# Gated cross-attention with a mixture of experts on one core: five expert tiles multiplied at the end of the attention program

## The chip, the cores and the metric

The kernel runs on one core of a Trainium2 chip. The metric is the device time of one execution in microseconds (us). Engines are named as the profile names them: PE is TensorE (matmuls), PEld its weight loads, DVE is VectorE, ACT is ScalarE, POOL is GpSimd, SP is SyncE, which here issues most DMAs.

## The reference: what is computed

```python
x = x + tanh(g_xattn) * xattn(layernorm(x), ctx)        # x: 4 x 2048 x 512, ctx: 4 x 77 x 512, 16 heads
x = x + tanh(g_ffn)   * ffn(layernorm(x))

def ffn(x):                                             # 8192 tokens of 512
    probs = softmax(x @ gate_w.T + gate_b)              # 8 true experts and 2 null ones
    weights, selected = top_k(probs, 2)
    true = weights * (selected < 8)
    norm = true / (true.sum(-1) or 1)
    return sum_k norm[k] * (x @ expert_w[selected[k]] + expert_b[selected[k]])
```

## The kernel before

The program has three parts, each a block with one instruction stream per engine. An engine enters a block only when all five have left the one before (a barrier: POOL gathers the other four, then releases them; it has the line of the block's start, L598 at the end of attention).

`fold_context` multiplies the context with the projection weights once. `attend` then goes over 64 tiles of 128 tokens in 64 turns and four more (`tail`, i = 64 to 67). A turn i works on several tiles: PE makes the scores of tile i (L908), the weighted sum `mix` of tile i-2 (L923) and the gate logits of tile i-4 (L955); DVE makes the probabilities of i-1, adds the residual of i-3 (`x_out`, L1152) and normalizes it (`y`, L1169), for which POOL computes the reciprocal root (`y_rstd`, L1499, x_moments); ACT does the exponentials and the f16 halves; SP turns p and y by DMA transposes (L819, L824, L809). In each stretch every engine goes through its list strictly in order. Every four tiles (a group, 16 in all) DVE ranks the tokens by expert in spread-out steps (place_1 to place_8), and POOL scatters eight rows of 128 entries each into a table in HBM (L1597). `placed` holds the counts so far. At the very end PE sums the counts (`totals`, L1002), and DVE makes the list of expert tiles from them (`count_tiles`, `find_tiles`, from L1609).

`run_experts` works through that list, first for the tokens' smaller choice (0), then for the other (1), each in passes of five tiles (RING = 5): one pass always, up to a counted number inside, and a last one. Per tile SP fetches the 128 table entries (L1769), DVE writes the token numbers (L1940), POOL gathers the rows by an indirect DMA (L1799), ACT normalizes (L1908), PE turns the tile with four f32 transposes (L1862), ACT and DVE make two f16 halves, PE does twelve 128x512 matmuls (L1875), DVE adds the bias and scales (L1963, L1988), and POOL scatters the result (L1820). PE starts the block with 14 matmuls whose result is not used (`WARM`, L1854). Choice 0 gathers and scatters into the second half of each token's row of `comb`; tiles are 128 tokens of one expert, the last of each expert filled up.

What sets the order around the change are the written-out step functions: `step` and `tail` of each engine in `attend`, and the first lines of each engine in `run_experts`. Of POOL there:

```python
listing.scatter(pool, table, 1, 2, 1, 2)
pool.wait_ge(cleared, 1)
for j in range(LEAD):                 # LEAD = 4
    gathers(choices[0], j, j)
listing.scatter(pool, table, 1, 3, 1, 2)
for t in range(GROUP):
    listing.scatter(pool, table, 0, t, 1, 2)
```

Of the kernel before, what the change touches and what calls it, by code (L numbers as in the profile page):

```python
# [71 lines left out]
FOLD_SLOTS = 4  # L72

# [54 lines left out]
def fold_context(nc, ident, identity, ident16, ones16, wq, wkv, wout, b_out, gate, g_xattn, ctx, arena, m_all, u_dram,  # L128
# [30 lines left out]
    with ExitStack() as stack:  # L159
# [3 lines left out]
        def sem(name):  # L163
            return stack.enter_context(nc.semaphore(name))
# [33 lines left out]
        wout_parts = sb("wout_parts", [P, PAIRS, 2, D], F16)  # L198
        u_stage = sb("u_stage", [P, US, 2, 2, D], F16)
        wq_parts = sb("wq_parts", [P, 2, PAIRS, D], F16)  # L200
        bias_parts = sb("bias_parts", [1, 2, D], F16)
# [386 lines left out]

def attend(nc, ident, ident16, x_in, u_dram, m_all, u_sb, comb, gate_b,
           ln, table, placed, ones16, expert_w, w_parts, listing, expert_b, expert_bias, bias_in):
# [5 lines left out]
    with ExitStack() as stack:  # L598
# [3 lines left out]
        def psum(name, shape, dt=F32):  # L602
            return stack.enter_context(nc.psum_tensor(name, shape, dt))

# [7 lines left out]
        x_res = sb("x_res", [P, 2, D])  # L612
# [3 lines left out]
        expd = sb("expd", [P, 2, COLS])  # L616
        total = sb("total", [P, 2, HEADS])
        inverse = sb("inverse", [P, 2, HEADS])
        p_parts = sb("p_parts", [P, 2, KT * P], F16)
# [42 lines left out]
        scores = [[psum(f"scores{s}_{k}", [P, 512]) for k in range(3)] for s in range(2)]  # L662
        mix = psum("mix", [P, D])
        routing = psum("routing", [P, 512])
# [104 lines left out]

        block = stack.enter_context(nc.Block())  # L770

        @block.sync
        def _(sp):
# [56 lines left out]

            def step(i, s):
# [63 lines left out]
        def _(pe):  # L895
# [81 lines left out]
            def step(i, s, q, turn):  # L977
# [8 lines left out]
                if live(i - 4):  # L986
                    gate(i - 4, s, q, turn)

# [15 lines left out]
            run(pe, step, tail)  # L1004

        @block.scalar
        def _(act):
# [48 lines left out]

            def step(i, s, q, turn):
# [17 lines left out]
            def tail(i, s, turn):  # L1075
# [6 lines left out]
                if i == TILES:  # L1082
                    high_w(i - 1, 1 - s)
                    exponent_gap(GROUPS - 2)
                if i == TILES + GROUP - 1:
# [7 lines left out]
        def _(dve):  # L1093
# [217 lines left out]
            def place_6(g):  # L1311
                after(g, 11)
                dve.tensor_tensor(placed[:], placed[:], hot_sum[:], ALU.add).then_inc(placed_ready, 1)
# [19 lines left out]
            def step(i, s, q, turn):  # L1333
                ps, pq, phase = delayed(s, q, turn)
                routed = pq - 1 if phase == 3 else pq - 2
                routes = live_group(routed)
                if live(i - 1):
                    probabilities(i - 1, 1 - s)
                if live(i - 3):
                    residual(i - 3, ps)  # L1340
                if phase == 2 and live_group(pq - 1):
                    keep_norms(pq - 1)
                if live(i - 3):
                    y_moments_of(i - 3, ps)
                if live(i + 2):
# [735 lines left out]
```

## Time and profile before

| | us |
|---|---|
| median of 3 runs (1365.13 to 1366.55) | 1365.33 |
| the profiled execution's own time | 1363.62 |
| its span in the trace | 1361.8 |
| PE busy (matmuls), 96% of the span | 1302.1 |
| DVE busy, 81% | 1109.2 |
| ACT busy, 55% | 752.8 |
| POOL busy, 50% | 686.4 |
| last instruction of the attention program on PE (its start) | 950.43 |
| first matmul of the expert program whose result is used (its start) | about 971.1 |

The span is counted from the first instruction; the times of the rows below are in us from there. A row of a timeline has start, duration, engine, line, operation, output and inputs, and in brackets how long the engine had been idle before it and what ended that. The chain of waits follows the end of the run back through whatever released each step. PEclk is the clock that TensorE was granted, 1.00 for 2.4 GHz and 0.50 for 1.2 GHz.

### The profile page before, as it was taken

To read this page: it belongs to the slowest core of one execution; us is meant where nothing else is said; L and a number is where in the kernel's file an instruction comes from. 1 tells how busy PE (TensorE), PEld (TensorE's weight loads), DVE (VectorE), ACT (ScalarE), POOL (GpSimd) and SP (SyncE) were. 2 spreads that over 40 slices of the span, in tenths; PEclk is the share of its full clock that TensorE was granted. 3 is DMA by queue.
4 is the path that set the end of the run, shared out by engine and by line. 5 is a ranking of instruction groups with operands and counts; after the bars stand their busy time and mean duration, and the time that the engine had idled before them with its cause. 6 is when DMAs were issued, how large, how long until landed. Compare 5 with 4: busy or idle time off the path is not lost. (4 is left out here: it accounts for less than half of the span.)

```text
span 1361.8 us, 30170 instructions
## 1 busy us (share of the span) xinstructions
PE 1302.1 (96%) x7339; PEld 674.7 (50%) x7340; DVE 1109.2 (81%) x2797; ACT 752.8 (55%) x2724; POOL 686.4 (50%) x645
## 2 busy tenths in 40 slices
PE   7999999999999999999999999996699988999997
PEld 5434555555555555555555555553355544555554
DVE  5776888998998998998998999987577765777775
ACT  4755666656656656656656656663444433444442
POOL 1501233446445455455455455445676755776674
PEclk9999999999999999999999999998799998999999
DMA  8144888778978778978778978877355535787773
GB/s 310 54 170 129 184 195 193 182 186 200 243 183 192 181 181 210 239 180 193 180 180 212 238 180 194 181 160 194 80 163 163 160 130 178 234 250 244 242 240 117
DMA packets 413298, 256.17 MB, mean 188 GB/s; under 512 B 338979, under 2 KB 350307, under 8 KB 413077
## 3 DMA queue, kind: packets, MB, share of 16 engines
q1 hardware_dynamic: 385365, 180.89, 54.9%
q0 software_dynamic: 27840, 74.18, 17.3%
q8 instruction: 41, 0.67, 0.2%
q14 instruction: 52, 0.43, 0.1%
HBM read 111.61 MB, written 75.01 MB: 137 GB/s over the span
## 5 line engine op out<-in xcount | busy, mean ns | idle before, releaser
L1023 ACT ACTIVATE expd<-scores,less 128x77 f32<-128x77 f32 x1024 | 317.4, 328 | 183.0 <-DVE less L1127 182.0
L908 PE MATMUL scores<-arena,zT 128*128 (+2 forms) x2304 | 414.8, 339 | 3.4 <-PEq L159 3.4
L923 PE MATMUL mix<-u_sb,pT 128*128 128x512 f16 x1728 | 383.5, 380 | 1.3 <-DMA pT<-p_parts 0.7
L1875 PE MATMUL out_bank<-arena,expert_yT 128*128 x1440 | 336.1, 384 | 0.0
L908 PEld LDWEIGHTS scores<-arena,zT 128*128 128x128 f16 x2304 | 220.7, 98 | 170.0 <-issue 5.8
L923 PEld LDWEIGHTS mix<-u_sb,pT 128*128 128x128 f16 x1728 | 168.8, 98 | 198.5 <-DVE x_out L1152 1.4
L1875 PEld LDWEIGHTS out_bank<-arena,expert_yT 128*128 128x128 f16 x1440 | 142.5, 99 | 148.1 <-issue 7.5
L1023 ACT ACTIVATION_READ_ACCUMULATOR expd<-scores,less 128x1 f32 x1024 | 213.5, 209 | 0.0
L1597 POOL DMA_INDIRECT table<-payload,row_i x128 | 159.7, 1248 | 60.1 <-issue 34.9
L1900 ACT CAST expert_yT<-yT_bank 128x512 f16<-128x512 f32 x120 | 70.2, 585 | 182.6 <-PE yT_bank L1862 180.9
L1494 POOL TENSOR_TENSOR z_parts<-z,z_parts 128x512 f16<-128x512 f32 x62 | 71.7, 1156 | 193.4 <-ACT z_parts L1014 193.4
L1988 DVE SCALAR_TENSOR_TENSOR result<-out_bank,slots,biased 128x512 f32<-128x512 f32 x120 | 90.1, 751 | 70.5 <-PE out_bank L1875 68.1
L1499 POOL TENSOR_TENSOR x_moments<-x_spread,minus_half 128x1 f32<-128x1 f32 x64 | 65.0, 1015 | 131.3 <-DVE x_spread L1162 131.2
L1953 DVE TENSOR_TENSOR expert_yT<-yT_bank,expert_yT 128x512 f16<-128x512 f32 x120 | 83.0, 691 | 46.6 <-ACT expert_yT L1900 45.0
L1125 DVE TENSOR_REDUCE top<-scores 128x5 f32<-128x385 f32 (+1 forms) x192 | 111.4, 580 | 3.5 <-PE scores L908 3.4
L1135 DVE SCALAR_TENSOR_TENSOR expd<-expd,inverse 128x1232 f32<-128x1232 f32 x64 | 92.3, 1442 | 2.2
L1799 POOL DMA_INDIRECT two_ring<-comb,token x66 | 71.1, 1077 | 45.1 <-issue 31.6
L1143 DVE TENSOR_TENSOR p_parts<-expd,p_parts 128x1232 f16<-128x1232 f32 x64 | 91.8, 1435 | 0.2 <-issue 0.2
L1862 PE MATMUL yT_bank<-ident,expert_y 128*128 128x128 f32 x480 | 74.7, 279 | 17.2 <-ACT expert_y L1908 13.7
L1820 POOL DMA_INDIRECT out_dram<-result,token_out x70 | 72.9, 1042 | 28.2 <-issue 19.0
L1862 PEld LDWEIGHTS yT_bank<-ident,expert_y 128*128 128x128 f32 x480 | 59.7, 143 | 44.2 <-ACT expert_y L1908 20.6
L1035 ACT CAST p_parts<-expd 128x1232 f16<-128x1232 f32 x64 | 77.7, 1214 | 0.0
(183 smaller groups left out, 1643.2 us busy)
## 6 DMA issues: line engine op xcount, KB each, us to landing
comb<-x_out SPq DMA_DIRECT2D x64, 512.0 KB, 3.2
x_ln<-in_x_dram SPq DMA_DIRECT2D x64, 256.0 KB
x_res<-in_x_dram SPq DMA_DIRECT2D x64, 256.0 KB, 2.8
w_raw<-in_L_ffn_expert_w_dram SPq DMA_DIRECT2D x64, 128.0 KB, 2.3
u_dram<-u_stage SPq DMA_DIRECT2D x12, 512.0 KB, 2.8
u_sb<-u_dram SPq DMA_DIRECT2D x6, 1024.0 KB, 7.6
arena<-in_L_xattn_w_kv_dram SPq DMA_DIRECT2D x4, 1024.0 KB, 7.5
slots<-table SPq DMA_DIRECT2D x150, 2.0 KB
```

What stands on the lines that cost most here:

```text
L908: last = pe.matmul(scores[s][k][:, 0:n], zT[:, s, zp, t, :], m, start=(t == 0 and (zp, mp) == PRODUCTS[0]), stop=(t == DT - 1 and (zp, mp) ...
L923: last = pe.matmul(mix[:], pT[:, s, pp, k, :], u_sb[:, k, up, :], start=(k == 0 and (pp, up) == PRODUCTS[0]), stop=False)
L1023: last = act.activation(expd[:, s, h * KEYS:(h + 1) * KEYS], scores[s][k][:, at:at + KEYS], ACT.Exp, bias=less[:, s, h:h + 1], scale=1.0 / ...
L1035: act.copy(p_parts[:, 0, 0:COLS], expd[:, s, :]).then_inc(p_hi_ready, 1)
L1125: dve.tensor_reduce(top[:, s, h0:h0 + nh], bank, AX_X, ALU.max).then_inc(top_ready, 1)
L1135: dve.scalar_tensor_tensor(e, e, P_SCALE, inverse[:, s].unsqueeze(2).broadcast_to([P, HEADS, KEYS]), ALU.mult, ALU.mult).then_inc(p_ready, 1)
L1143: dve.tensor_tensor(p_parts[:, 1, 0:COLS], expd[:, s, :], p_parts[:, 0, 0:COLS], ALU.subtract).then_inc(p_lo_ready, 1)
L1597: pool.indirect_dma_start(table, bass.IndirectOffsetOnAxis(ap=self.row_i[:, side, TOP_K * t + k:TOP_K * t + k + 1], axis=0), self.payload[ ...
L1862: last = pe.transpose(c.yT_bank[s][:, t, :], y[:, s, t * P:(t + 1) * P], ident[:])
L1875: last = pe.matmul(c.out_bank[s][:], yT[:, s, yp, t, :], w_of[:, bass.ds(e, 1), t, wp * D:(wp + 1) * D].rearrange("p a n -> p (a n)"), sta ...
L1953: dve.tensor_tensor(yT[:, s, 1], c.yT_bank[s][:], yT[:, s, 0], ALU.subtract).then_inc(c.y_lo_ready, 1)
L1988: dve.scalar_tensor_tensor(result[:, s, :], c.out_bank[buffer(s)][:], own, biased[:, buffer(s), :], ALU.mult, ALU.add).then_inc(c.result_r ...
```

## The change

Five expert tiles of choice 0 ("head" tiles) leave the expert program. PE sums the counts of the first twelve groups at the end of turn 60; in turn 61 DVE turns them into the first five full tiles (17 small operations in 13 steps); in turn 62 SP fetches their table entries, and DVE waits for these at the end of that turn; POOL gathers their rows in turns 63 and 64; ACT and POOL normalize and split them in turns 64 to 66; SP turns them by five DMA transposes, so PE does no transposes for them. PE multiplies all five at the end of the attention program, after `totals`. The expert program begins with their bias and scaling on DVE (two operations each) and their scatters on POOL; its list has five tiles of choice 0 fewer. The 14 unused matmuls are gone. Making the list for choice 1 moves from the start of the expert program to its first two tiles. For room, the semaphores of `fold_context` are cleared and used again, and all PSUM banks are named once for both programs. The core of the diff, by engine:

```diff
@@ PE @@
+                    if isinstance(i, int) and i == TILES - 3:
+                        pe.wait_ge(listing.head_done, 1)
                     gate(i - 4, s, q, turn)
+                if isinstance(i, int) and i == TILES - 4:
+                    pe.wait_ge(listing.head_placed_ready, GROUPS - 3)
+                    pe.matmul(totals, ones16[:], listing.head_placed[:], start=True, stop=True).then_inc(
+                        listing.head_counted, 1)
...
             run(pe, step, tail)
+            pe.wait_ge(w_lo_ready, TILES)
+            multiply_head(nc, pe, listing, banks, head_yT, w_parts, range(RING))
...
+def multiply_head(nc, pe, listing, banks, head_yT, w_parts, tiles):
+    w_of = w_parts.rearrange("p (e t) x -> p e t x", t=DT)
+    pe.wait_ge(listing.head_listed, 1)
+    chosen = nc.values_load_multi_w_load_instructions(
+        listing.head_expert[0:1, tiles.start:tiles.stop], (pe.engine,), min_val=0, max_val=EXPERTS - 1,
+        skip_runtime_bounds_check_because="head_9 clamps it")[1]
+    for j, e in zip(tiles, chosen):
+        pe.wait_ge(listing.head_yT_in[j], 16)
+        for t in range(DT):
+            for yp, wp in PRODUCTS:
+                last = pe.matmul(banks[HEAD_BANKS[j]][:], head_yT[:, j, yp, t, :],
+                                 w_of[:, bass.ds(e, 1), t, wp * D:(wp + 1) * D].rearrange("p a n -> p (a n)"),
+                                 start=(t == 0 and (yp, wp) == PRODUCTS[0]),
+                                 stop=(t == DT - 1 and (yp, wp) == PRODUCTS[-1]))
+        last.then_inc(listing.head_summed, 1)
@@ SP @@
+            def fetch_head():
+                sp.wait_ge(listing.head_listed, 1)
...
+            def turn_head(j):
+                sp.wait_ge(listing.head_lo_ready, j + 1)
+                sp.dma_start_transpose(out=head_yT[:, j].rearrange("p l t q -> p (l t) q"),
+                                       in_=head_parts(ln, j).rearrange("p l d -> p (l d)")).then_inc(listing.head_yT_in[j], 16)
...
                     turn_p_lo(i - 1, 1 - s)
+                if isinstance(i, int) and i == TILES - 2:
+                    fetch_head()
...
             for i in range(TILES, TILES + 4):
                 step(i, i % 2)
+                if i == TILES + 1:
+                    turn_head(0)
+                    turn_head(1)
+                if i == TILES + 2:
+                    turn_head(2)
+                    turn_head(3)
+                    turn_head(4)
@@ ACT, tail @@
+            def split_head(j):
+                act.wait_ge(listing.head_got[j], 16)
+                act.activation(head_y[j], listing.result[:, j, :], ACT.Identity, bias=listing.head_slots[:, j, 2:3],
+                               scale=listing.head_slots[:, j, 3:4]).then_inc(listing.head_y_ready, 1)
+                act.wait_ge(listing.head_y_ready, j + 1)
+                act.copy(head_parts(ln, j)[:, 0], head_y[j]).then_inc(listing.head_hi_ready, 1)
@@ DVE, the end of turn TILES - 2 (takes) @@
+                if takes:
+                    dve.wait_ge(listing.head_entry_in, 16 * RING)
+                    own = listing.head_slots[:, :, 0:1]
+                    dve.tensor_scalar(listing.head_token[:], own, 2.0, None, ALU.mult).then_inc(listing.head_token_ready, 1)
@@ POOL @@
             def tail(i, s, turn):
                 ps, t = 1 - s, (i - 3) % GROUP
                 if live(i - 3):
                     y_rstd(i - 3, ps, t)
                 if i == TILES:
+                    gather_head(3)
+                    gather_head(4)
+                if i == TILES + 2:
+                    low_head(2)
+                    low_head(3)
+                    low_head(4)
+                if i == TILES:
                     scatter(GROUPS - 3, ((1, 1), (2, 0), (2, 1), (3, 0)))
                 if i == TILES + 1:
                     scatter(GROUPS - 3, ((3, 1),))
                     scatter(GROUPS - 2, ((0, 0),), by_choice=True)
+                    low_head(0)
+                    low_head(1)
...
+                if isinstance(i, int) and i == TILES - 1:
+                    gather_head(0)
+                    gather_head(1)
+                    gather_head(2)
...
+            pool.memset(listing.result[:].rearrange("p s d -> p (s d)"), 0.0).then_inc(listing.result_clear, 1)
             run(pool, step, tail)
@@ run_experts: POOL, PE, DVE @@
             pool.wait_ge(cleared, 1)
+            scatter_head(0)
             for j in range(LEAD):
                 gathers(choices[0], j, j)
+            for j in range(1, R):
+                scatter_head(j)
...
-            for n in range(WARM):
-                again = pe.matmul(spare_bank[:], w_of[:, 0, n % DT, 0:P], w_of[:, 1, n % DT, 0:D], start=True, stop=True)
-            again.then_inc(warmed, 1)
...
+                elif c.k == 0 and j == 1:
+                    pe.wait_ge(listing.head_result, R)
...
+            finish_head(0)
+            finish_head(1)
             for j in range(R):
                 if j in (0, FIRST):
                     dve.wait_ge(entry_in[j // FIRST], 16 * (FIRST if j == 0 else R - FIRST))
                 name_token(choices[0], 0, j, j)
-            listing.find_tiles(dve, 1).then_inc(listing.listed, 1)
+            for j in range(2, R):
+                finish_head(j)
```

Three places of the order of instructions. First POOL in turns 63 to 66 (`x_moments` is y_rstd, `table<-payload` a scatter of the ranks, `x2` two alike). Before:

```order
L1503 TENSOR_TENSOR y_parts<-y,y_parts 128x512 [waits y_hi_ready]
L1597 DMA table<-payload,row_i 135168x4 [waits payload_ready,row_i_ready,placing]
L1597 DMA table<-payload,row_i 135168x4 x2
L1499 TENSOR_TENSOR x_moments<-x_spread,minus_half 128x1 [waits x_spread_ready]
L1597 DMA table<-payload,row_i 135168x4 [waits payload_ready,row_i_ready,placing]
L1597 DMA table<-payload,row_i 135168x4 x3
L1499 TENSOR_TENSOR x_moments<-x_spread,minus_half 128x1 [waits x_spread_ready]
L1597 DMA table<-payload,row_i 135168x4 [waits payload_ready,row_i_ready,placing] x2
L1499 TENSOR_TENSOR x_moments<-x_spread,minus_half 128x1 [waits x_spread_ready]
```

And now:

```order
L1863 DMA table<-payload,row_i 135168x4 x2
L1620 DMA result<-comb,head_token 128x512 [waits tanh_ready,gate_rows_in] x3
L1600 TENSOR_TENSOR x_moments<-x_spread,minus_half 128x1 [waits x_spread_ready]
L1620 DMA result<-comb,head_token 128x512 [waits tanh_ready,gate_rows_in] x2
L1863 DMA table<-payload,row_i 135168x4 [waits payload_ready,row_i_ready,placing]
L1863 DMA table<-payload,row_i 135168x4 x3
L1600 TENSOR_TENSOR x_moments<-x_spread,minus_half 128x1 [waits x_spread_ready]
L1863 DMA table<-payload,row_i 135168x4 [waits payload_ready,row_i_ready,placing] x2
L1627 TENSOR_TENSOR z_parts<-z,z_parts 128x512 [waits wout_hi_ready]
L1627 TENSOR_TENSOR arena<-z,arena 128x512 [waits wout_hi_ready]
L1600 TENSOR_TENSOR x_moments<-x_spread,minus_half 128x1 [waits x_spread_ready]
L1627 TENSOR_TENSOR arena<-x_ln,arena 128x512 [waits wout_hi_ready] x2
```

Three gathers now stand ahead of the y_rstd of tile 61, two more ahead of that of tile 62, and two subtractions (`low_head`) ahead of that of tile 63. (Waits are shown under the names of the cleared semaphores that are used again.)

Second SP in turns 65 to 67. Before:

```order
L809 DMA_TRANSPOSE yT<-y_parts 128x8x128 [waits y_hi_ready,y_lo_ready,gate_summed]
L778 DMA x_res<-in_x_dram 128x512 [waits x_out_ready]
L828 DMA comb<-x_out 256x1x512 [waits x_out_ready]
L809 DMA_TRANSPOSE yT<-y_parts 128x8x128 [waits y_hi_ready,y_lo_ready,gate_summed]
L828 DMA comb<-x_out 256x1x512 [waits x_out_ready]
L889 DMA u_sb<-in_L_ffn_expert_b_dram 128x4096 [waits u_read]
```

And now:

```order
L784 DMA x_res<-in_x_dram 128x512 [waits x_out_ready]
L834 DMA comb<-x_out 256x1x512 [waits x_out_ready]
L851 DMA_TRANSPOSE arena<-z_parts 128x8x128 [waits wout_scaled]
L851 DMA_TRANSPOSE arena<-arena 128x8x128 [waits wout_scaled]
L815 DMA_TRANSPOSE yT<-y_parts 128x8x128 [waits y_hi_ready,y_lo_ready,gate_summed]
L834 DMA comb<-x_out 256x1x512 [waits x_out_ready]
L851 DMA_TRANSPOSE arena<-arena 128x8x128 [waits wout_scaled] x3
```

The transpose of y of tile 62 (L815) stands behind two transposes of head tiles, each of which waits for a `low_head` on POOL.

Third POOL at the start of the expert program. Before:

```order
L1597 DMA table<-payload,row_i 135168x4
L1799 DMA one_ring<-comb,token 128x512 [waits cleared,token_ready_0]
L1799 DMA one_ring<-comb,token 128x512 [waits token_ready_0] x3
L1597 DMA table<-payload,row_i 135168x4 x5
L1741 TENSOR_LOAD inner_passes
```

And now:

```order
L1863 DMA table<-payload,row_i 135168x4
L2096 DMA comb<-result,head_token_out 16384x512 [waits gate_rows_in,head_result,cleared]
L2068 DMA one_ring<-comb,token 128x512 [waits token_ready_0] x4
L2096 DMA comb<-result,head_token_out 16384x512 [waits gate_rows_in,head_result] x4
L1863 DMA table<-payload,row_i 135168x4 x5
L2010 TENSOR_LOAD inner_passes
```

One scatter of a head tile stands ahead of the first gather, four more between the fourth gather and the fifth.

## Rows read from the trace of the kernel before

**Rows 1.** The chain of waits in the expert program: start, us, what

```profile
971.31 4.92 PE out_bank L1875 x12
...
982.28 0.44 PE yT_bank L1862 x4
982.72 2.59 PE out_bank L1875 x12
```

**Rows 2.** Groups of instructions on POOL, costliest first

```profile
L1503 POOL TENSOR_TENSOR y_parts<-y,y_parts 128x512 f16<-128x512 f32 x61 | 70.5, 1156 | 10.7 <-ACT y_parts L1042 10.7
...
L1799 POOL DMA_INDIRECT one_ring<-comb,token x50 | 54.3, 1086 | 32.0 <-issue 24.0 <-DVE token L1940 4.7 <-DVE token_out L1978 3.3
```

**Rows 3.** Timeline of PE, 924 to 969 us

```profile
924.95 6.00 PE L923 MATMUL mix<-u_sb,pT 128*128 128x512 f16 x27 [0.60 <-DVE x_out L1152]
...
939.43 0.18 PE L955 MATMUL routing<-gate_parts,yT 128*128 128x20 f16 x1 [0.45 <-DMA yT<-y_parts]
...
942.01 1.12 PE L939 MATMUL scores<-ident,y 128*128 128x128 f32 x4 [2.23 <-DVE y L1169]
...
950.43 0.19 PE L1002 MATMUL routing<-placed,ones 128*128 128x16 f16 x1 [1.91 <-DVE placed L1313]
959.50 4.53 PE L1854 MATMUL spare_bank<-arena 128*128 128x512 f16 x14 [8.88 <-PEq L598]
968.15 0.66 PE L1862 MATMUL yT_bank<-ident,expert_y 128*128 128x128 f32 x4 [4.12 <-ACT expert_y L1908]
```

**Rows 4.** Timeline of DVE, 911 to 939 us

```profile
911.58 0.25 DVE L1133 RECIPROCAL inverse<-total 128x16 f32<-128x16 f32 x1 [1.41 <-ACT expd L1023]
...
924.20 0.69 DVE L1152 SCALAR_TENSOR_TENSOR x_out<-mix,x_res 128x512 f32<-128x512 f32 x1 [0.40 <-PE mix L928]
...
938.83 0.69 DVE L1152 SCALAR_TENSOR_TENSOR x_out<-mix,x_res 128x512 f32<-128x512 f32 x1 [0.93 <-PE mix L928]
```

**Rows 5.** Busy time of each engine in a stretch of small DVE operations (columns PE, PEld, DVE, ...)

```profile
909.33:910.08 0.75, 0.75 (x5) 0.38 (x4) 0.75 (x10) 0.75 (x4) 0.00 (x1) 1.00 1.14 210
```

**Rows 6.** Timeline of POOL, 926 to 958 us

```profile
926.18 1.88 POOL L1499 TENSOR_TENSOR x_moments<-x_spread,minus_half 128x1 f32<-128x1 f32 x1 [0.25 <-DVE x_spread L1162]
...
933.40 0.69 POOL L1499 TENSOR_TENSOR x_moments<-x_spread,minus_half 128x1 f32<-128x1 f32 x1
...
940.81 0.57 POOL L1499 TENSOR_TENSOR x_moments<-x_spread,minus_half 128x1 f32<-128x1 f32 x1 [1.00 <-DVE x_spread L1162]
...
956.66 0.97 POOL L1597 DMA_INDIRECT table<-payload,row_i  x1 [0.30 <-issue]
```

**Rows 7.** Timeline of SP's DMA issues, 906 to 938 us

```profile
906.90 1.53 SPq L824 DMA_TRANSPOSE pT<-p_parts  x1
...
936.27 1.27 SPq L809 DMA_TRANSPOSE yT<-y_parts  x1
```

**Rows 8.** The chain of waits, 959 to 963 us

```profile
959.46 0.75 SPq L1775
...
961.00 1.67 DMA slots<-table
```

**Rows 9.** Busy time and granted clock (behind the five engines) in stretches around the restart

```profile
948.00:950.60 2.60, 0.54 (x6) 0.38 (x6) 2.08 (x21) 2.05 (x1) 1.99 (x3) 0.50 0.04 5
975.00:976.00 1.00, 1.00 (x4) 0.44 (x3) 0.00 (x0) 0.00 (x0) 0.70 (x2) 0.55 0.01 1
976.00:977.00 1.00, 1.00 (x8) 0.69 (x7) 0.66 (x1) 0.30 (x1) 0.96 (x1) 1.00 0.03 2
```

**Rows 10.** Timeline of POOL at the start of the expert program

```profile
963.76 1.05 POOL L1799 DMA_INDIRECT one_ring<-comb,token  x1 [2.60 <-DVE token L1940]
...
974.64 0.97 POOL L1597 DMA_INDIRECT table<-payload,row_i  x1 [0.30 <-issue]
975.92 1.04 POOL L1799 DMA_INDIRECT one_ring<-comb,token  x1 [0.30 <-issue]
```

**Rows 11.** Timeline of POOL, the start of the fold and of attention

```profile
1.26 4.39 POOL L570 MEMSET v_block<- 128x5120 f32 x1
...
126.57 1.16 POOL L1494 TENSOR_TENSOR z_parts<-z,z_parts 128x512 f16<-128x512 f32 x1 [5.07 <-ACT z_parts L1014]
```

More of the change, by code:

```diff
@@ L660, in attend @@
         kept_inv = sb("kept_inv", [P, GROUP])
-        scores = [[psum(f"scores{s}_{k}", [P, 512]) for k in range(3)] for s in range(2)]
-        mix = psum("mix", [P, D])
-        routing = psum("routing", [P, 512])
+        scores = [banks[3 * s:3 * s + 3] for s in range(2)]
+        mix, routing = banks[6:8]
         gate_bank = routing[:, 0:RANK0].rearrange("p (t l g) -> p t l g", t=GROUP, l=2)
@@ L1336, in step @@
                 routes = live_group(routed)
+                heads = isinstance(i, int) and i == TILES - 3
+                takes = isinstance(i, int) and i == TILES - 2
                 if live(i - 1):
@@ L1358, in step @@
                     y_spread_of(i - 3, ps, (phase + 2) % GROUP)
+                if heads:
+                    listing.head_3(dve)
+                if takes:
+                    listing.take_2(dve)
                 if live(i + 2):
@@ L1593, in __init__ @@
         self.steps = 0
+        self.head_placed = sb("head_placed", [P, TOP_K * EXPERTS], F16)
+        self.head_tokens = sb("head_tokens", [P, EXPERTS], I32)
+        self.head_tiles_i = sb("head_tiles_i", [P, EXPERTS], I32)
+        self.head_tiles = sb("head_tiles", [P, EXPERTS])
+        self.head_ends = [sb(f"head_ends{n}", [P, EXPERTS]) for n in range(3)]
+        self.head_past = sb("head_past", [P, RING, EXPERTS])
+        self.head_owner = sb("head_owner", [P, RING])
+        self.head_ahead = sb("head_ahead", [P, RING])
@@ new lines, in __init__ @@
+        self.head_left = sb("head_left", [P, EXPERTS])
+        self.taken = sb("taken", [P, TOP_K, EXPERTS])
+        self.taken_turn = sb("taken_turn", [P, TOP_K, EXPERTS])
+        self.held = sb("held", [P, TOP_K, EXPERTS])
+        self.head_expert = sb("head_expert", [P, RING], I32)
+        self.head_at = sb("head_at", [P, RING], I32)
+        self.head_slots = sb("head_slots", [P, RING, 4])
+        self.head_token = sb("head_token", [P, RING, 1], I32)
+        self.head_token_out = sb("head_token_out", [P, RING, 1], I32)
@@ new lines, in __init__ @@
+        self.head_got = [sem(f"head_got{s}") for s in range(RING)]
+        self.head_y_ready = sem("head_y_ready")
+        self.head_hi_ready = sem("head_hi_ready")
+        self.head_lo_ready = sem("head_lo_ready")
+        self.head_yT_in = [sem(f"head_yT_in{s}") for s in range(RING)]
+        self.head_summed = sem("head_summed")
+        self.head_biased = sem("head_biased")
+        self.head_result = sem("head_result")
+        self.head_put = [sem(f"head_put{s}") for s in range(RING)]
```

220 lines of the change are left out of this document (197 added, 23 removed).

## The prediction, made before the changed kernel was run

> **What bounds the kernel now.** The table of busy times says PE, 96% of the span, but the change works at the one place where PE is not busy, so the stretch between the two programs has to be read. The chain of waits comes first [rows 1]: in the expert program it runs through PE alone, four transposes (0.44 us) and twelve matmuls (2.59 us) per tile, so a tile costs 3.03 us and one fewer gives all of it back. The timeline of PE [rows 3] then shows the seam. Its last attention instruction (`totals`) starts at 950.43; it is idle 8.88 us until the barrier lets it go at 959.50, does 4.53 us of unused matmuls, and meets its first real work at 968.15. The barrier waited for POOL, whose last scatter ended at 956.66 + 0.97 = 957.63 [rows 6]: the release came 1.9 us later. The third thing to see is how tight the last turns are. PE's `mix` of tile 62 starts when DVE's x_out lets it [rows 3], and that x_out had waited only 0.40 us for PE [rows 4]: DVE has 0.4 us of slack. POOL starts the y_rstd of tile 62 without any wait [rows 6], so its queue has none. Work added there shows up.
>
> **Removed: five tiles.** POOL made 50 gathers for choice 0 [rows 2], ten passes of five. Taking five whole tiles off the list takes off exactly one pass: 5 x 3.03 = **-15.15 us**.
>
> **Added on DVE, turns 61 and 62.** Ten small operations take 0.75 us [rows 5], 0.08 each. Fifteen new ones stand ahead of the last maximum of turn 61, so ACT's exponentials and the next turn come 1.3 us later; turn 62 has six more (0.5). Worse is the wait for the table entries. SP issues the fetch behind the transpose of 906.90 + 1.53 us [rows 7], now 1.5 later, so at 909.9. It reads five numbers into registers (0.75), and the nearest case, the fetch of the expert program, needs about 4 us from there to the landing of the fifth entry (its first lands at 961.00 + 1.67, the others follow) [rows 8]. DVE goes on at about 915.0 where turn 63 began at 911.58 [rows 4]: +3.7, and less the 0.4 of slack, **+3.4 us** at x_out of tile 61 and the `mix` behind it.
>
> **Added on POOL.** An indirect DMA occupies it 1.09 us [rows 2], and the next starts 1.28 to 1.3 us after it (975.92 - 974.64, [rows 10]). Three gathers (3.9) go ahead of the y_rstd of tile 61, in which DVE's y waits, and DVE runs in order. Part is paid by the 1.88 us which that operation took, as against 0.6 elsewhere [rows 6]: x_out of tile 62 comes +6.1. Two more gathers (2.6) and nothing to hide them, as POOL was without slack at 933.40: y of tile 62 comes +8.9. `low_head` 0 and 1 cost 1.16 each [rows 2]; with them the y_rstd of tile 63 (940.81) comes +9.6.
>
> **Added on SP.** The transpose of y of tile 62 was issued at 936.27 [rows 7]. Now two head transposes of 1.3 us are ahead, and they wait for low_head, which sits on POOL behind the scatter that waits for place_8 of group 14, itself +8.9: low_head 1 ends near 949.5, the transpose is issued at 952 and lands 3.2 us later (939.43 - 936.27, [rows 3, 7]). PE's gate of tile 62 moves from 939.43 to 955.2, and since it is ahead of `turned` in PE's order, `turned` moves from 942.01 to 955.2: **+13.2 us** for everything that follows, `totals` included. This is the sum of delays in a chain, not of busy time: each engine stays idle much of it.
>
> **PE's 60 matmuls.** Behind `totals` (now 963.8) PE loads five expert numbers, 0.8 us by SP's load [rows 8], and multiplies. At full clock 5 x 2.59 = 12.95 us. The granted clock there was 0.50 [rows 9], and it comes back only under load: the 14 unused matmuls took 4.53 us [rows 3] where 14 x 0.216 = 3.0 would do, 1.5 lost; the first real tile took 4.92 where others take 2.59, 2.3 lost [rows 1]. Between the two I take 2.0: 15.0 us. PE leaves at 950.6 + 13.2 + 0.8 + 15.0 = 979.6. POOL is through near 971 and DVE's list as well, so the barrier now waits for PE, 979.6 instead of 957.63: **+22.0 us**. On TensorE's clock the Trainium skill, "TensorE: Matmul & The Clock Gate", Part 1, says that the number of matmuls at half rate after idle differs between runs, 6, 11 or 14 for one kernel. By 14 of them this term would be 1 us larger, an estimate from that page; the sum would then be 1377.7.
>
> **The restart.** The unused matmuls are gone at no cost: with them the first tile ran at half clock all the same (clock 0.55 until 976) [rows 1, 9]. The first gather was issued at 963.76 [rows 10]; two head finishes on DVE (four operations of about 0.75) end 1.1 us after the first entries arrive, and one head scatter is ahead of it on POOL: +1.1 to +1.6. The fifth gather (975.92) has four head scatters more ahead: +5.3 + 1.1 = +6.4. It fed the transposes that began at 982.28 [rows 1], with 1.9 us to spare (3.4 to land, 0.9 to normalize): **+4.5 us**, and the first gather's delay and the list for choice 1 (4.3 us of DVE, now between tiles 0 and 3) lie inside it. Bounds: 1.1 if the scatters overlap, 6.4 if nothing is to spare.
>
> **At nothing.** The cleared result buffer on POOL (128x2560, half of the 4.39 us that 128x5120 took) lies in the 5.07 us that POOL waits before its first z_parts [rows 11]; without that cover 2.2 us. Clearing semaphores at the first seam: one instruction, 0 to 0.5. One DVE copy per group, 13 x 0.08, spread under PE's work: 0 to 1. ACT has room: it is 55% busy.
>
> **Sum.** -15.15 + 22.0 + 4.5 = +11.35 us. The profiled execution's own time was 1363.62, so 1375.0; the median of the runs stands 1.7 above it: **1376.7 us**. The terms' bounds: tail 9.5 to 16 (without SP's queueing, or with slow landings), load 0.5 to 2.5, clock 1.0 to 3.6, restart 1.1 to 6.4. Together about +3.5 to +18.
>
> **The rivals.** A measurement of this kernel can tell about 0.2% (2.7 us) from no change.
> *Shorter tail.* The gathers and transposes find gaps that I took for none, and the tail grows 7 us instead of 13.2: +5.2, 1370.5. For it: PE's waits at 939.43, 942.01 and 950.43 are gaps [rows 3]. Against it: these are waits in the same chain.
> *Same.* Tail 3, restart 2: 1364.
> *Faster.* This is the purpose taken at its word: the 8.9 us gap and the unused matmuls are filled with real ones, the preparation hides. Without any tail PE ends at 950.6 + 15.8 = 966.4, which is 8.8 after POOL's 957.63. The barrier then costs 8.8 of the 15.15, so the break-even is at 6.3 us for tail and restart together. With 1 and 2 it is -3.35, 1362.0; with nothing, 1359. It needs DVE's wait for the entries (3.4 alone) to vanish and POOL's eight insertions too; rows 4 and 6 speak against it.
> *Clock.* The granted 0.50 stays for all 60 matmuls: 60 x 0.43 = 25.8 instead of 15, 1387.5. Against it: the first real tile ended at clock 1.00 [rows 9], and the 4.53 us of the unused matmuls are too few for half clock throughout (14 x 0.43 = 6.0) [rows 3].
> *It does not do what it says.* Fewer than five full tiles, so no pass falls: 1391.8. Three quarters of the tokens give over 30 tiles in choice 0, so hardly.
>
> **How the numbers follow.** The forecast 0.55, shorter tail 0.18, same 0.10, faster 0.12, clock 0.04, no pass fewer 0.01. The range 1364 to 1384 takes in the first three and the terms' bounds and leaves 0.17 out. Faster 0.12, same 0.10, slower 0.78.
>
> **What would show it.** In the profile after: turn 63's reciprocal on DVE near 915, ended by a DMA of head_slots just before; POOL's y_rstd of tile 61 near 933.5 without a wait; PE's gate of tile 62 waiting for the yT transpose until about 955; `totals` near 963.6; the 60 matmuls ending near 979.6, and the other engines' first instructions 1.9 us later, released by PE; 45 gathers for choice 0; a stall of PE of some 4 us at the transposes of the fifth tile, ended by ACT behind one_ring. Wrong would be: `totals` before 956 (then the tail is cheap and the change about neutral), a barrier released by POOL or DVE, or a restart no longer than before.

## The result, and the profile after

The changed kernel takes **1376.99 us** (median of 4 runs, 1376.04 to 1378.14), the kernel before 1365.23 beside it (4 runs): 1.0080 times as long, 95% interval 1.0065 to 1.0094, so 11.8 us slower. A second set, in another batch, gave 1377.38 against 1365.46, 1.0092 (1.0078 to 1.0105). The profiled execution of the changed kernel took 1378.14, the highest of its set; that of before (1363.62) lies below all of its set. So the two traces lie 14.5 apart, the medians 11.8. The experiments e5 to e8 ran as one batch in which the kernel before took 1401.21 (19 runs) and the expert program is what is longer in their traces, for a cause that stays open; of them only ratios and the stretch up to the seam are compared.

The head of the page after: PE is as busy as before, in a longer span.

```profile
span 1376.4 us, 30120 instructions
...
PE 1303.6 (95%) x7306; PEld 672.2 (49%) x7307; DVE 1107.9 (80%) x2821; ACT 752.8 (55%) x2724; POOL 698.2 (51%) x651
```

The executions are not in step even before the first instruction of the preparation in turn 61. DVE's reciprocal of that turn stands 1.66 us later here than before (the first line is before, the second after):

```profile
887.98 0.25 DVE L1133 RECIPROCAL inverse<-total 128x16 f32<-128x16 f32 x1 [1.14 <-ACT expd L1023]
...
889.64 0.25 DVE L1189 RECIPROCAL inverse<-total 128x16 f32<-128x16 f32 x1 [1.14 <-ACT expd L1063]
```

Of the 1.66, 1.31 are there at the first scores of attention (120.25 against 118.94). Most of it is scatter between executions: e3, which is the kernel before up to this point, has the same instruction at 889.72, and the changed kernel itself has it at 889.64 and, in e9, at 890.60. "Net" below means without this offset, which is 1.66 for this trace, 1.53 for e1, 1.74 for e3, 3.40 for e5, 2.62 for e9, 3.40 for e10 and 3.12 for e11. PE's timeline at the seam, to be laid beside [rows 3] and [rows 1]:

```profile
929.28 7.69 PE L955 MATMUL bank<-u_sb,pT 128*128 128x512 f16 x27 [3.37 <-DVE x_out L1208]
...
942.22 8.28 PE L955 MATMUL bank<-u_sb,pT 128*128 128x512 f16 x27 [3.23 <-DMA pT<-p_parts]
...
957.76 0.20 PE L987 MATMUL bank<-gate_parts,yT 128*128 128x20 f16 x1 [6.64 <-DMA yT<-y_parts]
...
957.99 1.09 PE L971 MATMUL bank<-ident,y 128*128 128x128 f32 x4
...
966.31 0.19 PE L1040 MATMUL bank<-placed,ones 128*128 128x16 f16 x1 [1.80 <-DVE placed L1371]
967.54 14.70 PE L1705 MATMUL bank<-arena 128*128 x60 [1.03 <-issue]
992.41 1.12 PE L2142 MATMUL bank<-ident,expert_y 128*128 128x128 f32 x4 [10.17 <-ACT expert_y L2188]
...
995.82 3.87 PE L2155 MATMUL bank<-arena,expert_yT 128*128 x12
...
1009.62 1.12 PE L2142 MATMUL bank<-ident,expert_y 128*128 128x128 f32 x4 [3.67 <-ACT expert_y L2188]
```

`totals` moved from 950.43 to 966.31, the first transposes of the expert program from 968.15 to 992.41, and a stall of 3.67 us stands at the fifth tile, where before had none (982.28). Between `totals` and the first transposes there are now 14.70 us of real matmuls, and still 10.17 us of idling behind them.

DVE and POOL show what came late. DVE waits for the table entries, then twice for POOL's reciprocal root; POOL runs without a wait from 925.39 until the end of the second y_rstd ([rows 4, 6] show before):

```profile
916.25 0.17 DVE L1506 TENSOR_SCALAR head_token<-head_slots 128x5 int32<-128x5 f32 x1 [4.08 <-DMA head_slots<-table]
...
936.15 0.60 DVE L1225 TENSOR_SCALAR y<-x_out,x_moments 128x512 f32<-128x512 f32 x1 [3.57 <-POOL x_moments L1600]
...
944.67 0.60 DVE L1225 TENSOR_SCALAR y<-x_out,x_moments 128x512 f32<-128x512 f32 x1 [3.28 <-POOL x_moments L1600]
```

```profile
931.05 1.83 POOL L1620 DMA_INDIRECT result<-comb,head_token  x1 [0.30 <-issue]
...
935.52 0.59 POOL L1600 TENSOR_TENSOR x_moments<-x_spread,minus_half 128x1 f32<-128x1 f32 x1
...
944.04 0.59 POOL L1600 TENSOR_TENSOR x_moments<-x_spread,minus_half 128x1 f32<-128x1 f32 x1
...
951.53 1.17 POOL L1627 TENSOR_TENSOR arena<-z,arena 128x512 f16<-128x512 f32 x1
...
972.70 0.97 POOL L1863 DMA_INDIRECT table<-payload,row_i  x1 [0.30 <-issue]
983.26 0.97 POOL L1863 DMA_INDIRECT table<-payload,row_i  x1 [9.59 <-POOLq L605]
```

SP's queue shows why PE's gate of tile 62 waits until 957.76: the transpose of y stands behind two head tiles (before it was issued at 936.27, [rows 7]).

```profile
951.63 1.26 SPq L851 DMA_TRANSPOSE arena<-z_parts  x1
952.93 1.34 SPq L851 DMA_TRANSPOSE arena<-arena  x1
954.47 1.23 SPq L815 DMA_TRANSPOSE yT<-y_parts  x1
```

The barrier: PE's last matmul ends at 967.54 + 14.70 = 982.24, and SP issues its first fetch of the expert program at 983.34, POOL its scatter at 983.26, after waiting 9.59 us for the barrier. POOL had been through at 973.67.

### The profile page after: what moved, and what is told of

It reads as the page before. It is cut to its first block and busy times, and to the rows that moved or that the text cites. A ratio compares the mean times of both kernels' runs of the same rounds, so it can differ in the third digit from the quotient of the medians.

```text
span 1376.4 us, 30120 instructions
## 1 busy us (share of the span) xinstructions
PE 1303.6 (95%) x7306; PEld 672.2 (49%) x7307; DVE 1107.9 (80%) x2821; ACT 752.8 (55%) x2724; POOL 698.2 (51%) x651
## 5 line engine op out<-in xcount | busy, mean ns | idle before, releaser
L940 PE MATMUL bank<-arena,zT 128*128 (+2 forms) x2304 | 414.9, 338 | 3.4 <-PEq L163 3.4
L1063 ACT ACTIVATE expd<-bank,less 128x77 f32<-128x77 f32 x1024 | 317.3, 328 | 182.8 <-DVE less L1183 181.7
L955 PE MATMUL bank<-u_sb,pT 128*128 128x512 f16 x1728 | 387.4, 382 | 6.6 <-DVE x_out L1208 3.4
L2155 PE MATMUL bank<-arena,expert_yT 128*128 x1380 | 323.1, 385 | 1.9 <-DVE token_out L2263 1.8
L940 PEld LDWEIGHTS bank<-arena,zT 128*128 128x128 f16 x2304 | 220.6, 98 | 170.0 <-issue 5.8
L955 PEld LDWEIGHTS bank<-u_sb,pT 128*128 128x128 f16 x1728 | 169.9, 98 | 206.7 <-issue 8.7
L1063 ACT ACTIVATION_READ_ACCUMULATOR expd<-bank,less 128x1 f32 x1024 | 213.5, 208 | 0.0
L2155 PEld LDWEIGHTS bank<-arena,expert_yT 128*128 128x128 f16 x1380 | 136.6, 99 | 144.5 <-issue 10.5
L2270 DVE SCALAR_TENSOR_TENSOR result<-bank,slots,biased 128x512 f32<-128x512 f32 x115 | 86.3, 751 | 67.0 <-PE bank L2155 64.6
L1181 DVE TENSOR_REDUCE top<-bank 128x5 f32<-128x385 f32 (+1 forms) x192 | 111.3, 580 | 4.1 <-PE bank L940 3.4
```

The source lines that it names most:

```text
L940: last = pe.matmul(scores[s][k][:, 0:n], zT[:, s, zp, t, :], m, start=(t == 0 and (zp, mp) == PRODUCTS[0]), stop=(t == DT - 1 and (zp, mp) ...
L955: last = pe.matmul(mix[:], pT[:, s, pp, k, :], u_sb[:, k, up, :], start=(k == 0 and (pp, up) == PRODUCTS[0]), stop=False)
L1063: last = act.activation(expd[:, s, h * KEYS:(h + 1) * KEYS], scores[s][k][:, at:at + KEYS], ACT.Exp, bias=less[:, s, h:h + 1], scale=1.0 / ...
L1181: dve.tensor_reduce(top[:, s, h0:h0 + nh], bank, AX_X, ALU.max).then_inc(top_ready, 1)
L2155: last = pe.matmul(c.out_bank[s][:], yT[:, s, yp, t, :], w_of[:, bass.ds(e, 1), t, wp * D:(wp + 1) * D].rearrange("p a n -> p (a n)"), sta ...
L2270: dve.scalar_tensor_tensor(result[:, s, :], c.out_bank[buffer(s)][:], own, biased[:, buffer(s), :], ALU.mult, ALU.add).then_inc(c.result_r ...
```

## The experiments

All are built on the changed kernel except e3. The first four ran beside the kernel before at 1365.69 (9 runs); the changed kernel was not in that batch, and "the change" stands for its 1376.99 and its ratio of 1.0080.

**e1: SP's transpose of y of tile 62 ahead of all head transposes.**

```diff
-                if i == TILES + 1:
+                if i == TILES + 2:
                     turn_head(0)
                     turn_head(1)
-                if i == TILES + 2:
                     turn_head(2)
```

> The changed kernel with SP's transposes of head tiles 0 and 1 put behind the transpose of y of tile 62. My theory (SP's queue is on the path): that transpose is issued near 947 instead of 954.5, as soon as y's low half is there (946.7 in the trace of the change), and PE's transposes of the last tile then wait for DVE's y alone: they start near 955.0 instead of 957.99. totals near 963.3, and the whole kernel 3.0 us faster than the change (about 1374). Rival (SP's queue is covered by y of tile 63, which is as late): 0 to 0.5 us.

Measured: 1374.69, ratio 1.0061 (1.0041 to 1.0081), 2.3 us less than the change. PE's transposes of y of tile 63 now wait for DVE and no longer for SP:

```profile
954.41 1.11 PE L970 MATMUL bank<-ident,y 128*128 128x128 f32 x4 [3.65 <-DVE y L1224]
...
962.87 0.20 PE L1039 MATMUL bank<-placed,ones 128*128 128x16 f16 x1 [1.90 <-DVE placed L1370]
```

So SP's queue is the last link of the tail, worth 3.6 us in the traces (957.99 to 954.41, net 3.5) and 2.3 in the runs. Behind it stands the delay that comes from POOL: DVE's y of tile 63 waits for POOL's y_rstd in e1 as well.

**e2: the fifth gather of the expert program ahead of four head scatters.**

```diff
-            for j in range(LEAD):
+            for j in range(R):
                 gathers(choices[0], j, j)
             for j in range(1, R):
                 scatter_head(j)
...
-                    if live(LEAD) and not (c.k == 0 and first_pass(r) and s + LEAD < LEAD):
+                    if live(LEAD) and not (c.k == 0 and first_pass(r) and s + LEAD < R):
```

> The changed kernel with the gather of the fifth tile of choice 0 put ahead of the four head scatters and five table scatters on POOL. My theory (POOL's queue makes PE's stall of 3.67 us at the fifth tile's transposes): that stall is gone, a smaller one of about 1 us may appear at the sixth tile, whose gather is now the first behind the nine scatters; the tile behind the stall also keeps the full clock. 3 to 4.5 us faster than the change. Rival (the gathers land late because of DMA load, or making choice 1's list on DVE is the limit): under 1.5 us.

Measured: 1372.65, ratio 1.0045 (1.0029 to 1.0061), 4.3 us less than the change. The stall of 3.67 us at the fifth tile is gone, and with it the lower clock behind it; small waits stay at the fifth and the sixth tile:

```profile
1008.76 2.76 PE L2155 MATMUL bank<-arena,expert_yT 128*128 x12 [1.48 <-ACT expert_yT L2180]
1012.24 0.66 PE L2142 MATMUL bank<-ident,expert_y 128*128 128x128 f32 x4 [0.72 <-ACT expert_y L2188]
```

**e3: the kernel before, with 60 unused matmuls at the end of PE's attention program.** This tests the barrier's term alone: no preparation, no tile less.

```diff
             run(pe, step, tail)
+            pe.wait_ge(w_lo_ready, TILES)
+            w_of = w_parts.rearrange("p (e t) x -> p e t x", t=DT)
+            for n in range(60):
+                held = pe.matmul(scores[1][0][:], w_of[:, 0, n % DT, 0:P], w_of[:, 1, n % DT, 0:D], start=True, stop=True)
+            held.then_inc(held_done, 1)
```

> The kernel before with 60 matmuls of 128x512 whose result is not used at the end of PE's attention program, behind the totals, and nothing else of the change. It measures the hold of the barrier alone. My theory: they run from about 951 to 966, the barrier opens 0.3 us after PE's last one instead of near 959.45, so the kernel is 6 to 7 us slower than before (1371 to 1372). Rival (PE's burst is hidden, since the barrier waits for POOL and DVE anyway): 0 to 1 us.

Measured: 1373.12, ratio 1.0050 (1.0032 to 1.0068): 7.4 us slower. PE's matmuls end at 967.80, and 0.33 us later it is in the next program:

```profile
952.28 15.52 PE L1009 MATMUL scores<-arena 128*128 128x512 f16 x60
968.13 3.18 PE L1860 MATMUL spare_bank<-arena 128*128 128x512 f16 x14 [0.33 <-PEq L598]
976.78 1.12 PE L1868 MATMUL yT_bank<-ident,expert_y 128*128 128x128 f32 x4 [5.47 <-ACT expert_y L1914]
```

The gap of 8.88 us [rows 3] is covered, and the rest of the 15.5 pushes the barrier: PE's next program starts net 6.9 later than before. So even with a free preparation this place costs about 7 of the 15.15 us that five tiles are worth.

**e4: 14 unused matmuls back at the start of the expert program,** into an idle bank.

> The changed kernel with the 14 unused matmuls put back at the start of PE's expert program (into a free bank). My theory: they cost and give nothing, since PE has over 9 us of waiting there and the clock is down again by the first real tile: within 0.5 us of the change. Rival (the restart runs at half clock for want of them): 1 to 3 us faster than the change.

Measured: 1378.13, ratio 1.0085 (1.0059 to 1.0111), 1.1 us more than the change, which is within the scatter. The matmuls take 3.18 us inside the wait for the first tile, and the first tile behind it is no faster for them: 4.54 us for twelve matmuls at a granted clock of 0.59 (998.5 to 1002.8), against 3.87 at 0.71 without them (995.9 to 999.6). Taking them out cost nothing.

The next four (e5 to e8) are the batch with the kernel before at 1401.21.

**e5: DVE waits for the table entries one turn later,** at the end of turn 63.

```diff
-                if takes:
+                if isinstance(i, int) and i == TILES - 1:
                     dve.wait_ge(listing.head_entry_in, 16 * RING)
```

> The changed kernel with DVE's wait for the head tiles' table entries, and the two operations behind it, at the end of turn 63 instead of turn 62. My theory: DVE's reciprocal of turn 63 starts near 912.5 instead of 916.5, the 3.4 us that PE waits for x_out of tile 61 goes, and all that follows comes some 4 us earlier, since POOL's three gathers start only behind the scatters of turn 63 in any case: about 1373, 4 us faster than the change. Rival (POOL's queue behind it is the limit, whatever DVE does): 0 to 1 us.

Measured: ratio 1.0080 (1.0051 to 1.0109), as the change. The expected 4 us did not show, but the interval is some 4 us wide to either side, so the runs do not decide. The trace does, for the stretch up to the seam. It lies 1.74 us behind that of the change already at DVE's reciprocal of turn 61 (891.38 against 889.64), and still at the `mix` of tile 61, the first line below (919.30 in the change's trace). This has to come off:

```profile
921.04 5.99 PE L955 MATMUL bank<-u_sb,pT 128*128 128x512 f16 x27
...
928.25 6.00 PE L955 MATMUL bank<-u_sb,pT 128*128 128x512 f16 x27 [0.60 <-DMA pT<-p_parts]
...
956.65 0.20 PE L987 MATMUL bank<-gate_parts,yT 128*128 128x20 f16 x1 [7.71 <-DMA yT<-y_parts]
```

```profile
934.49 0.59 POOL L1600 TENSOR_TENSOR x_moments<-x_spread,minus_half 128x1 f32<-128x1 f32 x1
```

DVE's wait of 4.08 us is gone. The `mix` of tile 62 (928.25 against 929.28), POOL's y_rstd of tile 61 (934.49 against 935.52), DVE's y of tile 62 (943.64 against 944.67) and PE's gate (956.65 against 957.76) all come 2.8 us earlier when the offset is taken off, and `totals` (965.59 against 966.31) 2.5. So the delay of DVE's wait runs through POOL to the end of the tail: POOL's y_low of turn 63 waits, by way of ACT, for the y that DVE makes later, and the scatters and gathers stand behind it. The later tokens held nothing up (DVE writes them at 923.99, the first gather starts at 929.90). Of the 2.5 us, 1.5 are left at the first transposes of the expert program (992.70 against 992.41), since the 60 matmuls took 15.77 us in this execution and 14.70 in the other.

**e6: three head tiles ahead of the barrier, two behind it.**

```diff
-            multiply_head(nc, pe, listing, banks, head_yT, w_parts, range(RING))
+            multiply_head(nc, pe, listing, banks, head_yT, w_parts, range(3))
@@ run_experts, PE @@
+            multiply_head(nc, pe, listing, banks, head_yT, w_parts, range(3, RING))
```

> The changed kernel with three of the five head tiles multiplied at the end of PE's attention program and two at the start of its expert program. My theory (the barrier is held by PE's 60 matmuls alone): the barrier opens two tiles earlier, 5 us, POOL being next at 1.4 us behind that, and the two tiles fit into PE's wait of 10 us at the restart: 5 us faster than the change, about 1372. Rival (the first real tile, or the result of tile 4, comes late because of them): 0 to 3 us faster.

Measured: ratio 1.0054 (1.0034 to 1.0074), some 3.7 us better than the change's 1.0080 (1.0065 to 1.0094); the intervals overlap a little, so the size is uncertain by a few us. The 24 matmuls lie in the wait for the first tile, whose 10.17 us fall to 3.49:

```profile
969.17 10.42 PE L1705 MATMUL bank<-arena 128*128 x36 [1.03 <-issue]
980.76 5.35 PE L1705 MATMUL bank<-arena 128*128 x24 [1.17 <-PEq L605]
989.59 0.66 PE L2144 MATMUL bank<-ident,expert_y 128*128 128x128 f32 x4 [3.49 <-ACT expert_y L2190]
...
1009.50 1.11 PE L2144 MATMUL bank<-ident,expert_y 128*128 128x128 f32 x4 [6.76 <-ACT expert_y L2190]
```

Part is given back at the fifth tile, where PE now waits 6.76 us for the gather that still stands behind the head scatters. How much of these 6.76 is the longer expert program of this batch is not known.

**e7 and e10: all delays of the tail moved at once.** DVE waits in the middle of turn 63; POOL gathers three tiles behind the y_rstd of tile 60 and ahead of y_low, two behind a scatter of turn 65, and all its subtractions follow the last y_rstd; SP turns all head tiles behind the y of tile 62. The same kernel ran in the batch of e5 to e8 (e7) and in a later one (e10, before 1365.46, 17 runs). Of the diff, the main part of POOL's:

```diff
@@ POOL, step; gathers 3 and 4 go behind scatter(GROUPS - 3, ((3, 1),)) @@
                     layernorm_rstd(i + 3, 1 - s)
+                if isinstance(i, int) and i == TILES - 1:
+                    gather_head(0)
+                    gather_head(1)
+                    gather_head(2)
                 if live(i - 3):
                     y_low(i - 3, ps)
...
@@ POOL, tail, i == TILES + 2 @@
+                    low_head(0)
+                    low_head(1)
                     low_head(2)
```

> The changed kernel with the head's preparation moved in the queues of the last turns, nothing taken away: DVE's wait for the entries in the middle of turn 63, three gathers ahead of the y_low of tile 60, two behind the last scatter of group 13 in turn 65, all five low_head behind the y_rstd of tile 63, all five head transposes behind the transpose of y of tile 62. My theory (the delay of 14 us of the totals is queue order and not work): the totals come 2 to 4 us later than before the change instead of 14, and the kernel takes about 1366, 11 us less than the change. Rival (the engines lack the time for the work, wherever it stands): 1370 or more.

> The same kernel as e7_tail_moves. Its trace shows totals at 959.20 where the change has 966.31, and the first transposes at 986.10 where the change has 992.41, so 6.3 to 7.1 us should come off the change: ratio to the kernel before 1.003, about 1370 us. The rival, that the delays of the tail only shift into the slow restart, has it within 2 us of the change.

Measured: ratio 1.0026 (1.0007 to 1.0045) and 1.0017 (1.0001 to 1.0032). e10 took 1368.57 against 1377.38 for the changed kernel itself in that batch (e9), 8.8 us less, where e7's expectation was 11. `totals` in e10's trace, and then in e9's:

```profile
949.72 1.12 PE L970 MATMUL bank<-ident,y 128*128 128x128 f32 x4 [1.06 <-DVE y L1224]
...
958.20 0.20 PE L1039 MATMUL bank<-placed,ones 128*128 128x16 f16 x1 [1.80 <-issue]
```

```profile
967.16 0.20 PE L1040 MATMUL bank<-placed,ones 128*128 128x16 f16 x1 [1.80 <-DVE placed L1371]
```

`totals` comes 9.0 us earlier, net 9.7. At the first transposes of the expert program 7.6 of the 9.0 are left (985.36 against 992.92), since the 60 matmuls took 15.91 us in e10 and 14.64 in e9, and the two profiled executions lie 6.3 apart (1371.08 and 1377.38). What is left of the tail against the kernel before is 958.20 - 950.43 less the offset of 3.40, so 4.4 us, where 2 to 4 were expected. It is not the same in every execution: e7, the same kernel, has `totals` at 959.20, net 7.8, and the 12 runs of e10 scatter from 1363.24 to 1372.76; see the last section.

**e9: the changed kernel itself, as the base of that batch.**

> The changed kernel itself, unaltered, as the base of this batch, since the batch with the four last kernels ran on a chip whose expert program was slower as a whole (1401 us for the kernel before). Ratio to the kernel before: 1.008 if the chip runs at the earlier speed, 1376 to 1378 us. If what the change costs depended on the slower state, the ratio would leave 1.0065 to 1.0094.

Measured: 1377.38 (5 runs), ratio 1.0092 (1.0078 to 1.0105), as expected.

**e8 and e11: e7, with the fifth gather early and two head tiles behind the barrier.**

> All together: the moves of the tail, three head tiles before the barrier and two behind it, and the fifth gather ahead of the head scatters. My theory, the sum: tail +3, hold of the barrier +1 (PE's three tiles end about when POOL's last scatter does), restart +1.5, five tiles -15.15, so some 10 us faster than before: 1355 to 1358. Rival (the costs overlap, each repair uncovers the next wait): 1361 to 1365.

> The same kernel as e8_all. Its trace has the first transposes at 977.65, which is 9.5 us later than in the kernel before, and five tiles fewer (-15.15): without a stall at the fifth tile 5.7 us below the kernel before, ratio 0.996, about 1360 us. In the slower batch that stall was 5.11 us and the ratio 1.0002. If the stall belongs to the kernel (a gather or a finish that is late) and not to that batch, the ratio stays at 1.000; if it belongs to the batch, it is gone here.

Measured: e8 1.0002 (0.9983 to 1.0022), a miss (some 10 us below the kernel before were expected, which would be a ratio near 0.993), and e11, in the later batch, **0.9955 (0.9942 to 0.9968)**: 1358.82 (6 runs, 1357.96 to 1365.60), 6.6 us less than the kernel before (17 runs) and 18.6 less than the change. PE in e11, whose trace is that of its slowest run:

```profile
962.56 10.82 PE L1703 MATMUL bank<-arena 128*128 x36 [1.05 <-issue]
974.46 5.35 PE L1703 MATMUL bank<-arena 128*128 x24 [1.08 <-PEq L605]
983.52 1.12 PE L2142 MATMUL bank<-ident,expert_y 128*128 128x128 f32 x4 [3.71 <-ACT expert_y L2188]
...
1002.65 0.66 PE L2142 MATMUL bank<-ident,expert_y 128*128 128x128 f32 x4 [1.04 <-ACT expert_y L2188]
```

The last line is the sixth tile, not the fifth: with the fifth gather early the fifth tile's transposes do not wait in e8 or e11, and the stall of 5.11 us that e11's expectation puts at the fifth is at the sixth in e8's trace. It is 1.04 us here, so it went with that batch. The parts add up roughly: 8.8 (e10) + 4.3 (e2) + 3.7 (e6) = 16.8, measured 18.6, each part uncertain by 2 to 3 us. A reason for a remainder would be that the split no longer moves the wait to the fifth tile as in e6; no run isolates it.

## Why the prediction was right

The forecast was 1376.7 and +11.35; measured 1376.99 and +11.8. Its steps, one by one, net of the offset:

- *Removed, -15.15.* One pass of five tiles is gone: 45 gathers for choice 0.
- *DVE's wait, +3.4 at the mix of tile 62.* The wait for the entries ended at 916.25, net 914.6, where 915.0 was forecast, and the mix started 4.33 - 1.66 = 2.7 later. Right in kind and 0.7 too large. The prediction carried the delay on into the +6.1 and +8.9 of the next tiles, and e5 bears this out: without the wait the whole chain comes 2.5 to 2.8 us earlier.
- *POOL's insertions.* y_rstd of tile 61 at 935.52 (net 933.9, forecast 933.5), without a wait. That of tile 62 stands at 944.04, net +9.0, where +8.9 was forecast for y. Two errors cancel in this: DVE's 0.7 less, and five gathers that took 7.3 us of POOL (931.05 to 935.52, 936.11 to 938.96) instead of 6.5.
- *The two subtractions.* The prediction has low_head 1 end near 949.5 and y_rstd of tile 63 +9.6. Its own delay of +8.9 for the scatter that waits for place_8 gives more: that scatter started at 938.83 before and at 949.43 after (net 947.8),

```profile
938.83 0.98 POOL L1597 DMA_INDIRECT table<-payload,row_i  x1 [3.24 <-DVE payload L1330]
...
949.43 0.99 POOL L1863 DMA_INDIRECT table<-payload,row_i  x1 [3.58 <-DVE payload L1388]
```

  and with 0.98 and twice 1.16 behind it low_head 1 ends at 951.0, which is what was measured (951.53 + 1.17 = 952.70, net 951.0). y_rstd of tile 63 came at 952.94, net +10.5. That the transpose of y was still forecast right, at 952, is luck: the time between the end of low_head 1 and its issue was taken as 2.5 us and was 1.8.
- *SP's queue, `turned` at 955.2, +13.2.* Measured 957.99, net 956.3: +14.3. The transpose was issued at 954.47, net 952.8, forecast 952. e1, e5 and e10 confirm the chain: without SP's queueing 2.3 us come back, without DVE's wait 2.5 at `totals` in the trace, with all three moved 8.8.
- *60 matmuls, 0.8 + 15.0.* Measured 1.03 (at `totals` 966.31 + 0.19 = 966.50 to 967.54) and 14.70. The granted clock was 0.79 on average in the first 7.4 us, which holds both levels, and 1.00 (2.4 GHz) in the rest:

```profile
967.60:975.00 7.40, 7.40 (x28) 3.07 (x29) 5.25 (x17) 3.10 (x1) 4.96 (x4) 0.79 0.18 70
975.00:982.00 7.00, 7.00 (x34) 3.09 (x32) 0.00 (x0) 0.52 (x1) 0.00 (x0) 1.00 0.00 0
```

  The Trainium skill ("TensorE: Matmul & The Clock Gate", Part 1) gives 6, 11 or 14 matmuls at half rate for one and the same kernel. By the 14 the stretch would be 16 us, an estimate from that page; this trace stays below it, and e1, e2 and e9 with 14.50 to 14.64 too, while the same 60 took 16.03 in e4, 15.77 in e5 and 15.91 in e10. So both ends occur, and the trace agrees with the page that the number varies.
- *The barrier, +22.0.* It waits for PE, as forecast. The 1.9 us between the last instruction and the release were wrong for PE: they are 0.3, as e3 shows too. Net release 982.24 + 0.3 - 1.66 = 980.9, where before had 959.50: +21.4; the tail's extra 1.1 and the shorter release nearly cancel.
- *Restart, +4.5.* The stall at the fifth tile is 3.67 us, and its transposes moved by 27.34 in all (982.28 to 1009.62), which is 4.3 more than the release's 23.0. The fifth gather was issued at 1005.01, 6.1 behind its old distance from the release where 6.4 was forecast, and the slack of 1.9 took the rest off. What the prediction did not count is the clock behind the stall: the tile took 4.83 us in the chain, where 2.59 is usual [rows 1].

```profile
1009.62 1.12 PE bank L2142 x4
1010.73 4.83 PE bank L2155 x12
```

  That is 2.2 more, and e2, which removes the stall and the lower clock and keeps small waits, gains 4.3.
- *At nothing.* The unused matmuls were indeed worth nothing (e4). The cleared buffer, the semaphores and the copies per group are not separated: all traces of the changed kernel stand between 0.9 and 3.4 us behind before at turn 61, but so does e3 (1.74), which has none of them.
- *The bounds.* The four terms' own bounds add up to +2.9 and +19.3, not to +3.5 and +18; the stated range of 1364 to 1384 holds nearly all of it.

The sum of the traces closes: 27.34 - 15.15 = 12.2 up to the fifth tile, offset included, and 2.2 behind it make 14.4 of the 14.5 between the two executions. Net of the offset that is some 12.8, against 11.35 forecast; that the medians differ by 11.8 and the forecast missed the median by only 0.3 us is partly luck, with 2.2 us of lower clock left out and a release 1.6 us too long. Right was the reading that the gap of 8.88 us is smaller than what was put into it, and that the last turns have no slack; the rival that the preparation hides fell by `totals` at net 964.7. It falls for this placement only: e11, with the same work in other places, is 6.6 us faster than the kernel before.

## What to carry to other kernels

An idle gap ahead of a barrier holds as much work as it is long and no more (here 8.9 us for 15.7), and work behind the barrier can sit in the wait for the first gather; split it between the two. Insertions into in-order queues cost by their place: one wait of DVE, five gathers and two subtractions on POOL and two transposes on SP, moved by a few instructions so that the last tiles' chain does not stand behind them, gave 8.8 us without one operation fewer. And lay two traces on a common instruction ahead of the change before comparing times: e5's raw times show 1.0 us where the chain had moved by 2.8.

## What the runs showed of the hardware

- A wait of PE in the middle of attention costs twice, once as a wait and once by a lower granted clock behind it. The `mix` of tile 62 and 63, 6.00 us before [rows 3], took 7.69 and 8.28 behind waits of 3.4 and 3.2 us, at a granted clock of 0.77 and 0.71:

```profile
929.30:936.80 7.50, 7.50 (x27) 3.06 (x28) 3.90 (x15) 0.79 (x1) 6.07 (x7) 0.77 0.89 203
942.30:950.20 7.90, 7.90 (x27) 3.10 (x27) 3.32 (x23) 5.24 (x8) 3.83 (x5) 0.71 0.56 184
```

  In e5, behind 0.60 us, the first of them took 6.00 again; in e10 a wait of 2.69 us was enough for 7.67. This extra time was hardly on the path here: y of tile 62 waits for POOL long after its `mix`, and POOL's y_rstd of tile 63 waited only 0.23 us for what follows from the `mix` of that tile.
- The block barrier opens 0.3 us after PE's last matmul (e3) and 1.9 us after POOL's last scatter [rows 3, 6]. Whether an indirect DMA in flight or POOL's part in the barrier makes the difference was not tried.
- How fast SP's DMA transposes of p are in the last turns varies, and what is left of e10's tail varies with it. PE waited for one of them 2.69 us in e10 and 3.23 in e8, with `totals` net 4.4 and 4.3 behind before, but 5.20 us in e11 and 6.38 in e7, with `totals` net 7.8 behind in both:

```profile
930.20 3.34 SPq L825 DMA_TRANSPOSE pT<-p_parts  x1
```

```profile
932.66 8.46 PE L954 MATMUL bank<-u_sb,pT 128*128 128x512 f16 x27 [5.20 <-DMA pT<-p_parts]
```

  That would fit the scatter of e10's runs. The cause is not shown. The new gathers run in this turn, but they are not needed for a slow transpose: the kernel before has one of 2.75 us with no gather of rows beside it.

```profile
917.40 2.75 SPq L824 DMA_TRANSPOSE pT<-p_parts  x1
```
